# Vision tower on one core: scores of attention in the feed-forward before it, values behind them in another bank pair

## The chip, the cores and the metric

The kernel runs on one core of a Trainium2 chip. The metric is the time of one execution on the device, in microseconds (us). It was run three times: 1611.28, 1611.56 and 1613.82 us, median 1611.56. A profiled execution is a fourth one.

## What is computed

64 images (2 channels, 104x104) become 170 tokens of 128 numbers each (169 patches of 8x8 and a class token), and go through three stages. The reference, cut to what matters (helpers and reshapes left out):

```python
h = tok(x, gamma, beta, W, b)               # normalise 5 shifted copies, 8x8 convolution
h = concatenate([cls_tok, h], axis=1)       # 170 tokens per image
h = h + graph(layernorm(h), ...)            # two graph convolutions over 128 features, projection Wp
h = h + block(layernorm(h), ...)

def block(x):                               # 2 heads of 64, 8 experts of 512
    hx = layernorm(x) * ln_g + ln_b
    q, k, v = hx @ Wq, hx @ Wk, hx @ Wv     # per head
    q, k = l2norm(q) * 8 * qn_g, l2norm(k) * 8 * kn_g
    attn = softmax(where(causal, q @ k.T / 8, lowest))
    y = (attn @ v) @ Wo
    gate = softmax(y @ gate_W + gate_b)
    hid = gelu(y @ W1[e] + b1[e])           # for each of 8 experts, all tokens
    return sum_e gate[e] * (hid @ W2[e] + b2[e])
```

## The kernel before

The features lie on the 128 partitions, the tokens on the free axis. After the convolutions of all images, the 64 images are worked off in 16 groups of 4 (`NB`), 680 tokens each. A group passes a front end (second normalisation, graph, queries and keys), the attention and the feed-forward part. The front end of a group runs inside the feed-forward part of the groups in front of it, so one loop turn holds the feed-forward part of group g-1, the queries and keys of g, the start of g+1, and then the attention of g.

The feed-forward part has 32 slots (`SLOTS`: 8 experts, 4 chunks of 128 hidden features). In a slot TensorE multiplies six fp16 matmuls of 340 columns into a bank pair of `hid_ps` (`experts_in`, L869), ScalarE applies gelu once or twice (L564, L569), VectorE casts and subtracts to get the high and low fp16 parts (L1211, L1213), and three slots later (`LAG`) TensorE multiplies six more into `eo_ps` (`experts_out`, L886). After each fourth chunk VectorE weighs the expert's result with its gate (L1225, two halves) and GpSimd's queue adds it to the output in DRAM (L401). Slots 32 to 34 have no `experts_in` left. Fixed tables (`LN2_SLOTS`, `GATE_SLOTS`, `QK_SLOTS`, `EARLY_SLOTS`) say in which slot each front-end step runs. Every engine executes its own list in that order; semaphores join them.

PSUM is cut into four pairs of banks: two are `hid_ps`, one is `eo_ps`, one (`fr_ps`) belongs to the front end. `fr_ps` is last read in the feed-forward part by ScalarE's four relus of the next group but one (L485, slots 28 to 31), and the graph's products (`graph`, steps "plain" and 0 to 3, through `both`, L664) write it during the attention.

TensorE's order around the attention of group g is: `values` (L768) of two tokens' tiles at a time, in slots 32, 33, 34 and once more after them, each block of six fp16 matmuls into a quarter of `hid_ps`; `scores` of samples 0 and 1 (L783, and the mask, L787), which wait until ScalarE has copied the values of their bank out (`values_evac`, L518); "plain" and graph product 0 of group g+1; `scores` of samples 2 and 3; graph products 1 and 2; the transposes of the probabilities (`turn_probs`, L798) of samples 0 and 1; graph product 3; then weighing (`weigh`, L810), transposes and the projection (`project`, L817) by turns, the mean of the graph's result, and the gate logits (L853).

VectorE's order: the last expert's weighing in slot 34, then `maxima` of samples 0 and 1 and of 2 and 3 (two reductions, L1120, and nbias, L1123), `normalise` (L1128, L1135) of samples 0 and 1, the copy of the turned probabilities (`turned`, L1142) of sample 0, and so on by turns. ScalarE copies the values out, then runs 16 exponentials (`exps`, L528), each with a read of its sum.

In group 0 nothing lies in front of the attention (`later` is false), in group 15 there is no next group's graph (`ahead` is false).

Of the kernel before, what the change touches and what calls it, by code (L numbers as in the profile page):

```python
# [36 lines left out]
NB = 4  # L37
# [44 lines left out]
def vit_tower(nc, cells1, cells0, pack_a, pack_b, edge, w1, w2, out):  # L82
    with ExitStack() as ctx:
# [326 lines left out]
        def _(act):  # L410
# [100 lines left out]
                                         root[:, 2 * TILES:4 * TILES].unsqueeze(2).broadcast_to([QC, H * TILES, DH]),  # L511
                                         ACT.Copy).then_inc(wide_ready, 1)

            def values_evac(g, b, later):
                act.wait_ge(vp_ps, g * NB + b + 1)
                if b == 0 and later:
                    act.wait_ge(tmp_ready, g * E - 1)
                nc.scalar.activation(vp[:, b * 2 * D:(b + 1) * 2 * D], hid_ps[b // 2][0:QC, b % 2, 0:2 * D],  # L518
                                     ACT.Copy).then_inc(vp_ready, 1)

            def exps(g, b):

                act.wait_ge(nb_ready, g * (NB // 2) + b // 2 + 1)
# [18 lines left out]
                nc.scalar.activation(y32[:, j * TH:(j + 1) * TH], hid_ps[1][:, j, 0:TH], ACT.Copy).then_inc(y_ready, 1)  # L542

            def attention(g, later, ahead):
                for b in range(NB):
                    values_evac(g, b, later)
                for b in range(NB):
                    exps(g, b)
                nc.scalar.activation(primer[:, :], eps[0:1, 0:1], ACT.Gelu_apprx_tanh)
                o_evac(g, 0)  # L550
                y_evac(g, 0)
                o_evac(g, 1)
                y_evac(g, 1)
                if ahead:
                    graph(g + 1, "sq2")
                act.wait_ge(lg_step, 3 * (g + 1))
                nc.scalar.activation(lge[:, :], lg[:, :], ACT.Tanh, scale=0.5).then_inc(lge_ready, 1)
# [46 lines left out]
        def _(pe):  # L604
# [103 lines left out]
                    pe.wait_ge(xnl_ready, g + 1)  # L708
                    of_xn(adj_h[:, :], adj_l[:, :]).then_inc(g_ps, 1)

            def graph(g, step):
                if step == "plain":
                    pe.wait_ge(h1_ready, 4 * (g + 1))
                    of_xn(plain_h[:, :], plain_l[:, :], stop=False)
                if step in range(4):
                    last = both(gcn_m[:, step * D:(step + 1) * D], two(h1[:, step * T:(step + 1) * T]),
                                start=False, stop=(step == 3))
                    if step == 3:
                        last.then_inc(gcn_ps, 1)
                if step == "mean2":  # L720
                    pe.wait_ge(h2_ready, g + 1)
                    both(mean_m[:, :], tokens(g)).then_inc(mean2_ps, 1)
                if step == "var2":
                    pe.wait_ge(sq2_ready, g + 1)
                    means(sq).then_inc(var2_ps, 1)
                if step == "cast":
                    cast_roots(g, "ln2")
# [28 lines left out]
                if step == "cast":  # L756
                    cast_roots(g, "qk")

            def values(g, b, later):

                if b == 0 and later:
                    pe.wait_ge(hhi_act, his(g, 0) - 1)
                if b == 2 and later:
                    pe.wait_ge(hhi_act, his(g, 0))
                for k in range(2):
                    t = 2 * b + k
                    for n, (x_part, w_part) in enumerate(((xh_h, wv_h), (xh_l, wv_h), (xh_h, wv_l))):
                        last = mm(hid_ps[b // 2][0:QC, b % 2, k * D:(k + 1) * D],  # L768
                                  x_part[:, t * QC:(t + 1) * QC], w_part[:, :], start=(n == 0), stop=(n == 2))
                last.then_inc(vp_ps, 1)  # L770

            def scores(g, m):

                if m == 0:
                    pe.wait_ge(kn_ready, g + 1)
                pe.wait_ge(vp_ready, g * NB + 2 * m + 2)
                for b in (2 * m, 2 * m + 1):
                    ps = score_ps_at(b)
                    for c in range(2):
                        w = (c + 1) * QC  # L780
                        for h in range(H):
                            p = slice(h * DH, (h + 1) * DH)
                            mm(ps[:, h, c * QC:c * QC + w], qs[p, (2 * b + c) * QC:(2 * b + c + 1) * QC],  # L783
                               kb[p, b * TOK:b * TOK + w], start=(b == 2 * m and c == 0), stop=False)
                for h in range(H):
                    corners = hid_ps[m][0:QC, h, 0:2 * 3 * QC].rearrange("p (i j n) -> p i j n", i=2, j=3)[:, :, 0:3:2, :]
                    last = mm(corners, identb[:, :], mask[:, :].unsqueeze(1).unsqueeze(1).broadcast_to([QC, 2, 2, QC]),  # L787
                              start=False, stop=True)
                last.then_inc(score_ps, 1)
# [12 lines left out]
            def weigh(g, b):  # L802

                pe.wait_ge(pt_ready, g * NB + b + 1)
                for k in range(2):
                    for h in range(H):
                        v0 = b * 2 * D + k * D + h * DH
                        p0 = h * 3 * QC + k * TOK
                        y0 = (b % 2) * TOK
                        last = mm(hid_ps[0][h * DH:(h + 1) * DH, b // 2, y0 + k * QC:y0 + TOK], vp[:, v0:v0 + DH],  # L810
                                  pt[b % 2][0:QC, p0:p0 + TOK - k * QC], start=(k == 0), stop=(k == 1))
                last.then_inc(pv_ps, 1)
# [11 lines left out]
            def attention(g, later, ahead):  # L824
                def graph_of(*steps):
                    if ahead:
                        for step in steps:
                            graph(g + 1, step)

                for b in range(LAG if later else 0, NB):  # L830
                    values(g, b, later)
                scores(g, 0)
                graph_of("plain", 0)
                scores(g, 1)
                graph_of(1, 2)
                turn_probs(g, 0, later)
                turn_probs(g, 1, later)
                graph_of(3)
# [53 lines left out]
            def ffn(g, ahead):  # L892
                for slot in range(SLOTS + LAG):
                    if slot < SLOTS:
# [7 lines left out]
                        if ahead:  # L902
                            for step in steps_in(EARLY_SLOTS, slot):
                                early(g + 2, step)
                    else:
                        values(g + 1, slot - SLOTS, True)
                    if slot >= LAG:
                        experts_out(g, slot - LAG)

# [27 lines left out]
        def _(dve):  # L937
# [206 lines left out]
            def y_parts(g, j):  # L1144
# [4 lines left out]
                dve.wait_ge(yh_ready, 2 * g + j + 1)  # L1149
                v.tensor_tensor(yl[:, half], y32[:, half], yh[:, half], ALU.subtract).then_inc(yl_ready, 1)  # L1150

            def attention(g, later, ahead):
                maxima(g, 0)
                maxima(g, 1)
                normalise(g, 0)
                normalise(g, 1)
                turned(g, 0)
# [76 lines left out]
            def ffn(g, successor=True, ahead=True, later=True):  # L1234
                for slot in range(SLOTS + LAG):
                    expert_slot(g, slot, later)
                    for step in steps_in(GATE_SLOTS, slot):
                        gates(g, step, later)
                    if successor:
                        for step in steps_in(LN2_SLOTS, slot):  # L1240
                            graph(g + 1, step)
                        for step in steps_in(QK_SLOTS, slot):
                            queries_keys(g + 1, step)
                    if ahead:
                        for step in steps_in(EARLY_SLOTS, slot):
                            early(g + 2, step)
# [70 lines left out]
```

## Time and profile before

| what | value |
|---|---|
| three runs, median | 1611.56 us |
| profiled execution | 1615.64 us, its span 1613.8 us |
| TensorE (PE) busy | 1495.1 us, 93% of the span |
| VectorE (DVE) busy | 1211.3 us, 75% |
| ScalarE (ACT) busy | 1099.5 us, 68% |
| GpSimd (POOL) busy | 227.3 us, 14% |
| mean granted TensorE clock | 0.963 of full speed |

The span is what the profiler saw between the first and the last instruction; the time holds what lies around it as well. "Busy" counts every instruction from its start to its end; TensorE's instructions overlap and their ends are modelled, so a TensorE that is always busy need not be at its peak. A timeline merges instructions of one line that follow each other: the number behind the x says how many. A square bracket at a row's end says how long the engine was idle before it and what ended that. PEld is TensorE's loading of weights. The granted clock is 1.00 at full speed (2.4 GHz) and 0.50 at half. An fp32 matmul shows as two matmul instructions.

### The profile page before, as it was taken

What the parts mean: (1) busy time and instruction counts of PE and PEld (TensorE: products, weight loads), DVE (VectorE), ACT (ScalarE), POOL (GpSimd) and SP (SyncE); (2) the same over time, 40 slices, a digit from 0 to 9 for tenths busy, and PEclk for the clock granted to TensorE, in tenths of its full rate; (3) what the DMA queues carried; (4) which work ended last, traced back from release to release, by engine and by line L of the source; (5) the groups of instructions that cost most, each with busy time, mean ns of one, the idle gap of its engine ahead of it and who ended that gap; (6) DMA issues with size and microseconds to landing.
All of it is one profiled execution on the core that took longest, in us unless ns stands there. A gap on an engine that the chain in (4) does not pass through costs nothing.

```text
span 1613.8 us, 31251 instructions
## 1 busy us (share of the span) xinstructions
PE 1495.1 (93%) x10837; PEld 1020.8 (63%) x10837; DVE 1211.3 (75%) x2510; ACT 1099.5 (68%) x1879; POOL 227.3 (14%) x213
## 2 busy tenths in 40 slices
PE   5993589999999999999999999999999999999998
PEld 3551356666666666666666666666666666667665
DVE  7994358787868778787878787887878787877665
ACT  2321157777777777777777777777777777777766
POOL 5376101010110101010101101010101010110101
PEclk8995589999999999999999999999999999999979
DMA  5312004243333333241423333233324242433323
GB/s 189 116 65 79 9 5 110 36 104 43 97 51 95 42 89 52 59 80 26 112 35 104 43 95 47 92 43 91 49 45 94 33 109 38 104 43 97 53 88 53
DMA packets 33714, 113.48 MB, mean 70 GB/s; under 512 B 5008, under 2 KB 5008, under 8 KB 31120
## 3 DMA queue, kind: packets, MB, share of 16 engines
q0 software_dynamic: 18432, 44.57, 20.5%
q1 hardware_dynamic: 14960, 67.71, 11.4%
q10 hardware_dynamic: 288, 0.77, 0.1%
q8 instruction: 18, 0.29, 0.1%
q14 instruction: 16, 0.13, 0.0%
HBM read 62.56 MB, written 50.48 MB: 70 GB/s over the span
## 4 chain that ended last, share of the span: by engine, by line
PE 59%; DVE 28%; issue 7%; ACT 4%; DVEq 1%; DMA 1%; POOL 0%; POOLq 0%; ACTq 0%
PE pair L886 20%; PE pair L869 17%; PE pair L664 7%; DVE area L1213 5%; PE pair L650 4%; DVE area L1135 3%; DVE root_t L1055 2%; PE pair L783 2%; DVE area L1142 2%; DVE area L1225 2%; PE pair L692 1%; PE pair L676 1%; PE pair L817 1%; PE pair L739 1%; PE pair L810 1%
## 5 line engine op out<-in xcount | busy, mean ns | idle before, releaser
L564 ACT ACTIVATE area<-pair,pack_b_sb 128x680 f32<-128x680 f32 x512 | 422.8, 828 | 220.4 <-PE pair L869 217.8
L1213 DVE TENSOR_TENSOR area<-area 128x680 f16<-128x680 f32 x512 | 441.1, 864 | 149.3 <-ACT area L569 143.8
L886 PE MATMUL pair<-area,ws 128*128 128x340 f16 x3072 | 529.8, 307 | 12.9 <-DVE area L1225 11.8
L869 PE MATMUL pair<-area,ws 128*128 128x340 f16 x3072 | 527.1, 308 | 0.0
L886 PEld LDWEIGHTS pair<-area,ws 128*128 128x128 f16 x3072 | 284.3, 98 | 168.8 <-DVE area L1225 44.1
L869 PEld LDWEIGHTS pair<-area,ws 128*128 128x128 f16 x3072 | 297.8, 98 | 143.7 <-issue 0.2
L569 ACT ACTIVATE area<-pair,pack_b_sb 128x680 f16<-128x680 f32 x384 | 316.4, 824 | 0.0
L401 POOL DMA_DIRECT2D tower_out<-area x128 | 109.7, 857 | 1266.8 <-DVE area L1225 1205.3
L1225 DVE SCALAR_TENSOR_TENSOR area<-pair,pack_b_sb,area 128x340 f32<-128x340 f32 x256 | 134.0, 565 | 28.9 <-PE pair L886 19.9
L528 ACT ACTIVATE area<-pair,nbias,root 85x85 f32<-85x85 f32 (+1 forms) x256 | 112.4, 464 | 22.4 <-DVE nbias L1123 22.4
L650 PE MATMUL pair<-area,pack_a_sb 128*128 128x512 f32 (+1 forms) x260 | 97.1, 533 | 18.4 <-DVE area L1006 18.4
L650 PEld LDWEIGHTS pair<-area,pack_a_sb 128*128 128x128 f32 x260 | 50.7, 198 | 62.5 <-issue 42.9
L664 PE MATMUL pair<-area,gcn_m 128*128 128x340 f32 x256 | 83.4, 461 | 0.0
L1120 DVE TENSOR_REDUCE mx<-pair 85x4 f32<-85x340 f32 x64 | 41.0, 680 | 55.8 <-PE pair L787 55.8
L1006 DVE TENSOR_TENSOR area<-area,pack_a_sb 128x832 f32<-128x832 f32 x65 | 75.1, 1218 | 7.7 <-DMA pack_a_sb<-pack_a 6.3
L1211 DVE CAST area<-area 128x680 f16<-128x680 f32 x128 | 65.6, 513 | 19.7 <-ACT area L564 14.4
L451 ACT ACTIVATE ht<-pair 128x832 f32<-128x832 f32 x13 | 22.5, 1730 | 75.9 <-PE pair L650 75.9
L485 ACT ACTIVATE area<-pair,pack_b_sb 128x680 f32<-128x680 f32 x64 | 59.2, 935 | 20.2 <-PE pair L664 19.7
L373 POOL TENSOR_TENSOR area<-area 128x896 f32<-128x896 f32 x13 | 57.0, 4383 | 39.0 <-DMA area<-cells 38.0
L664 PEld LDWEIGHTS pair<-area,gcn_m 128*128 128x128 f32 x256 | 47.4, 195 | 18.0 <-issue 1.4
L798 PE MATMUL pair<-ident,area 85*85 85x85 f32 x384 | 45.4, 256 | 13.4 <-DVE area L1135 13.4
L1135 DVE TENSOR_SCALAR area<-area,rs 85x85 f32<-85x85 f32 (+1 forms) x256 | 55.7, 278 | 2.3
(182 smaller groups left out, 1640.7 us busy)
## 6 DMA issues: line engine op xcount, KB each, us to landing
tower_out<-area POOLq DMA_DIRECT2D x128, 340.0 KB, 4.6
area<-gate_scratch SPq DMA_DIRECT2D x16, 1360.0 KB, 9.9
area<-gate_scratch SPq DMA_DIRECT2D x16, 1020.0 KB, 7.1
area<-cells SPq DMA_DIRECT2D x14, 448.0 KB, 3.7
tower_out<-ht SPq DMA_DIRECT2D x16, 340.0 KB, 2.3
area<-gate_scratch SPq DMA_DIRECT2D x16, 340.0 KB, 4.4
area<-cells SPq DMA_DIRECT2D x13, 416.0 KB, 4.3
area<-w SPq DMA_DIRECT2D x1, 2048.0 KB, 10.1
```

The source lines that it names most:

```text
L401: pool.dma_start(out[:, g * T:(g + 1) * T], tmp[e % 2], accum_op=ALU.add).then_inc(out_done, 16)
L528: nc.scalar.activation(probs[:, b * SCORE + o0:b * SCORE + o0 + w], score_ps_at(b)[:, h, c * QC:c * QC + w], ACT.Exp, bias=nbias[:, n:n + ...
L564: nc.scalar.activation(two(hid[slot % NHID]), halves(hid_ps[slot % 2]), ACT.Gelu_apprx_tanh, bias=col(COL_B1 + slot)).then_inc(hid_ready, 1)
L569: nc.scalar.activation(two(hh[slot % NPART]), halves(hid_ps[slot % 2]), ACT.Gelu_apprx_tanh, bias=col(COL_B1 + slot)).then_inc(hhi_act, 1)
L650: last = mm(flat(conv_ps(p))[:, a:b], conv_w[:, s * D:(s + 1) * D], xg[p % 2][s][:, a:b], start=(s == 0), stop=(s == SHIFTS - 1))
L664: last = mm(fr_ps[:, j, 0:TH], lhs, rhs[:, j, :], start=start, stop=stop)
L869: last = mm(hid_ps[slot % 2][:, j, 0:TH], lhs[:, w], rhs[:, j * TH:(j + 1) * TH], start=(i == 0), stop=(i == 2))
L886: last = mm(eo_ps[:, j, 0:TH], lhs[:, w], rhs[:, j * TH:(j + 1) * TH], start=(m % CH == 0 and i == 0), stop=(m % CH == CH - 1 and i == 2))
L1006: v.tensor_tensor(xg[p % 2][s].rearrange("p (j b) -> p j b", b=B), src[:, c0 * B:(c0 + NP) * B].rearrange("p (j b) -> p j b", b=B), gv, AL ...
L1135: last = v.tensor_scalar(p, p, rs[:, n:n + 1], None, ALU.mult)
L1213: v.tensor_tensor(hl[slot % NPART], hid[slot % NHID], hh[slot % NPART], ALU.subtract).then_inc(hlo_ready, 1)
L1225: v.scalar_tensor_tensor(tmp[e % 2][:, j * TH:(j + 1) * TH], eo_ps[:, j, 0:TH], b2_s[:, e:e + 1], gbc[:, e * T + j * TH:e * T + (j + 1) * ...
```

## The change

The functions `scores` and `maxima` of group g+1 are now called in slots 32 and 33 of the feed-forward part of group g, where `values` stood on TensorE. All four blocks of values are made in the attention itself, behind slot 34, in `fr_ps` instead of `hid_ps`, once the relus have read it. VectorE (`values_out`) copies them out in two copies of 85x512 behind the last expert's weighing, where ScalarE had four copies of 85x256. "plain" waits for these copies, and so does each weighing. The scores wait for ScalarE's second gelu of slot 30 or 31 instead of for the values. In group 0 the scores and maxima of all samples stand ahead of the values.

```diff
--- before.py
+++ after.py
@@ -511,13 +511,6 @@
                                          root[:, 2 * TILES:4 * TILES].unsqueeze(2).broadcast_to([QC, H * TILES, DH]),
                                          ACT.Copy).then_inc(wide_ready, 1)
 
-            def values_evac(g, b, later):
-                act.wait_ge(vp_ps, g * NB + b + 1)
-                if b == 0 and later:
-                    act.wait_ge(tmp_ready, g * E - 1)
-                nc.scalar.activation(vp[:, b * 2 * D:(b + 1) * 2 * D], hid_ps[b // 2][0:QC, b % 2, 0:2 * D],
-                                     ACT.Copy).then_inc(vp_ready, 1)
-
             def exps(g, b):
 
                 act.wait_ge(nb_ready, g * (NB // 2) + b // 2 + 1)
@@ -542,8 +535,8 @@
                 nc.scalar.activation(y32[:, j * TH:(j + 1) * TH], hid_ps[1][:, j, 0:TH], ACT.Copy).then_inc(y_ready, 1)
 
             def attention(g, later, ahead):
-                for b in range(NB):
-                    values_evac(g, b, later)
+                if later:
+                    act.wait_ge(tmp_ready, g * E - 1)
                 for b in range(NB):
                     exps(g, b)
                 nc.scalar.activation(primer[:, :], eps[0:1, 0:1], ACT.Gelu_apprx_tanh)
@@ -708,9 +701,11 @@
                     pe.wait_ge(xnl_ready, g + 1)
                     of_xn(adj_h[:, :], adj_l[:, :]).then_inc(g_ps, 1)
 
-            def graph(g, step):
+            def graph(g, step, after=False):
                 if step == "plain":
                     pe.wait_ge(h1_ready, 4 * (g + 1))
+                    if after:
+                        pe.wait_ge(vp_ready, 2 * g)
                     of_xn(plain_h[:, :], plain_l[:, :], stop=False)
                 if step in range(4):
                     last = both(gcn_m[:, step * D:(step + 1) * D], two(h1[:, step * T:(step + 1) * T]),
@@ -756,24 +751,23 @@
                 if step == "cast":
                     cast_roots(g, "qk")
 
-            def values(g, b, later):
-
-                if b == 0 and later:
-                    pe.wait_ge(hhi_act, his(g, 0) - 1)
-                if b == 2 and later:
-                    pe.wait_ge(hhi_act, his(g, 0))
+            def values(g, b, ahead):
+
+                if b == 0 and ahead:
+                    pe.wait_ge(h1_ready, 4 * (g + 2))
                 for k in range(2):
                     t = 2 * b + k
                     for n, (x_part, w_part) in enumerate(((xh_h, wv_h), (xh_l, wv_h), (xh_h, wv_l))):
-                        last = mm(hid_ps[b // 2][0:QC, b % 2, k * D:(k + 1) * D],
+                        last = mm(fr_ps[0:QC, b // 2, (2 * (b % 2) + k) * D:(2 * (b % 2) + k + 1) * D],
                                   x_part[:, t * QC:(t + 1) * QC], w_part[:, :], start=(n == 0), stop=(n == 2))
                 last.then_inc(vp_ps, 1)
 
-            def scores(g, m):
+            def scores(g, m, later):
 
                 if m == 0:
                     pe.wait_ge(kn_ready, g + 1)
-                pe.wait_ge(vp_ready, g * NB + 2 * m + 2)
+                if later:
+                    pe.wait_ge(hhi_act, his(g, 0) - 1 + m)
                 for b in (2 * m, 2 * m + 1):
                     ps = score_ps_at(b)
                     for c in range(2):
@@ -802,6 +796,7 @@
             def weigh(g, b):
 
                 pe.wait_ge(pt_ready, g * NB + b + 1)
+                pe.wait_ge(vp_ready, 2 * g + b // 2 + 1)
                 for k in range(2):
                     for h in range(H):
                         v0 = b * 2 * D + k * D + h * DH
@@ -825,14 +820,14 @@
                 def graph_of(*steps):
                     if ahead:
                         for step in steps:
-                            graph(g + 1, step)
-
-                for b in range(LAG if later else 0, NB):
-                    values(g, b, later)
-                scores(g, 0)
-                graph_of("plain", 0)
-                scores(g, 1)
-                graph_of(1, 2)
+                            graph(g + 1, step, after=True)
+
+                if not later:
+                    for m in range(NB // 2):
+                        scores(g, m, later)
+                for b in range(NB):
+                    values(g, b, ahead)
+                graph_of("plain", 0, 1, 2)
                 turn_probs(g, 0, later)
                 turn_probs(g, 1, later)
                 graph_of(3)
@@ -902,8 +897,8 @@
                         if ahead:
                             for step in steps_in(EARLY_SLOTS, slot):
                                 early(g + 2, step)
-                    else:
-                        values(g + 1, slot - SLOTS, True)
+                    elif slot - SLOTS < NB // 2:
+                        scores(g + 1, slot - SLOTS, True)
                     if slot >= LAG:
                         experts_out(g, slot - LAG)
 
@@ -1149,9 +1144,16 @@
                 dve.wait_ge(yh_ready, 2 * g + j + 1)
                 v.tensor_tensor(yl[:, half], y32[:, half], yh[:, half], ALU.subtract).then_inc(yl_ready, 1)
 
+            def values_out(g, k):
+                dve.wait_ge(vp_ps, g * NB + 2 * k + 2)
+                v.tensor_copy(vp[:, k * 4 * D:(k + 1) * 4 * D], fr_ps[0:QC, k, :]).then_inc(vp_ready, 1)
+
             def attention(g, later, ahead):
-                maxima(g, 0)
-                maxima(g, 1)
+                if not later:
+                    for m in range(NB // 2):
+                        maxima(g, m)
+                for k in range(NB // 2):
+                    values_out(g, k)
                 normalise(g, 0)
                 normalise(g, 1)
                 turned(g, 0)
@@ -1234,6 +1236,8 @@
             def ffn(g, successor=True, ahead=True, later=True):
                 for slot in range(SLOTS + LAG):
                     expert_slot(g, slot, later)
+                    if successor and 0 <= slot - SLOTS < NB // 2:
+                        maxima(g + 1, slot - SLOTS)
                     for step in steps_in(GATE_SLOTS, slot):
                         gates(g, step, later)
                     if successor:
```

## Rows read from the trace of the kernel before

**Rows 1.** The page, part 4: shares of the chain that ended last, by engine.
```profile
PE 59%; DVE 28%; issue 7%; ACT 4%; DVEq 1%; DMA 1%; POOL 0%; POOLq 0%; ACTq 0%
```
**Rows 2.** Timeline of PE, first transposes of groups 1 and 14 (start, duration, what).
```profile
310.41 0.68 PE L798 MATMUL pair<-ident,area 85*85 85x85 f32 x6 [0.35 <-DVE area L1135]
...
1451.80 0.68 PE L798 MATMUL pair<-ident,area 85*85 85x85 f32 x6 [0.41 <-DVE area L1135]
```
**Rows 3.** Timeline of PE around the attention of group 8.
```profile
736.62 1.03 PE L886 MATMUL pair<-area,ws 128*128 128x340 f16 x6
737.48 0.27 PE L768 MATMUL pair<-wv_h,area 128*85 128x128 f16 x2
...
737.82 1.03 PE L886 MATMUL pair<-area,ws 128*128 128x340 f16 x6
...
743.03 0.75 PE L664 MATMUL pair<-pack_a_sb,plain_h 128*128 128x340 f16 x4
...
745.14 1.12 PE L783 MATMUL pair<-area 64*85 64x85 f32 x16
...
746.51 2.45 PE L664 MATMUL pair<-area,gcn_m 128*128 128x340 f32 x8
749.37 0.68 PE L798 MATMUL pair<-ident,area 85*85 85x85 f32 x6 [0.41 <-DVE area L1135]
...
754.88 0.66 PE L810 MATMUL pair<-area 85*64 85x170 f32 x8 [0.33 <-DVE area L1142]
...
759.98 1.89 PE L869 MATMUL pair<-area,ws 128*128 128x340 f16 x12
```
**Rows 4.** Waits of PE: total us, times, longest us.
```profile
PE pair L798 <- DVE area L1135: 13.4, 32, 3.1
```
**Rows 5.** Timeline of DVE around the attention of group 8.
```profile
739.42 0.87 DVE L1213 TENSOR_TENSOR area<-area 128x680 f16<-128x680 f32 x1 [1.38 <-ACT area L569]
741.09 1.05 DVE L1225 SCALAR_TENSOR_TENSOR area<-pair,pack_b_sb,area 128x340 f32<-128x340 f32 x2 [0.79 <-DMA tower_out<-area]
...
746.71 1.28 DVE L1120 TENSOR_REDUCE mx<-pair 85x4 f32<-85x340 f32 x2 [2.00 <-PE pair L787]
...
748.15 0.17 DVE L1128 RECIPROCAL rs<-sm 85x4 f32<-85x4 f32 x1
...
750.15 0.68 DVE L1142 COPY area<-pair 85x510 f32<-85x510 f32 x1
...
754.15 1.27 DVE L1142 COPY area<-pair 85x510 f32<-85x510 f32 x2
```
**Rows 6.** Timeline of ACT, group 8: the first exponential.
```profile
744.74 0.42 ACT L528 ACTIVATE area<-pair,nbias,root 85x85 f32<-85x85 f32 x1 [1.30 <-DVE nbias L1123]
```
**Rows 7.** Timelines of PE, then DVE, around the attention of the last group.
```profile
1521.71 1.03 PE L886 MATMUL pair<-area,ws 128*128 128x340 f16 x6
...
1532.73 0.96 PE L798 MATMUL pair<-ident,area 85*85 85x85 f32 x6 [3.11 <-DVE area L1135]
...
1538.74 1.16 PE L798 MATMUL pair<-ident,area 85*85 85x85 f32 x6
1539.83 1.12 PE L810 MATMUL pair<-area 85*64 85x170 f32 x8
...
1547.59 0.73 PE L869 MATMUL pair<-area,ws 128*128 128x340 f16 x2
...
1531.59 0.17 DVE L1128 RECIPROCAL rs<-sm 85x4 f32<-85x4 f32 x1 [0.47 <-ACT area L528]
```
**Rows 8.** Busy time by stretch: us, PE, PEld, DVE, ACT, POOL, then PEclk, DMA share, GB/s.
```profile
1534.00:1538.00 4.00, 3.52 (x22) 2.93 (x24) 3.77 (x15) 3.98 (x15) 0.00 (x0) 0.50 0.00 0
...
1550.00:1560.00 10.00, 10.00 (x60) 6.00 (x58) 6.38 (x12) 7.70 (x11) 0.00 (x0) 0.83 0.19 73
```
**Rows 9.** Timeline of PE in the attention of group 0.
```profile
213.93 1.12 PE L783 MATMUL pair<-area 64*85 64x85 f32 x16 [1.64 <-ACT area L518]
...
223.20 0.68 PE L798 MATMUL pair<-ident,area 85*85 85x85 f32 x6 [0.28 <-DVE area L1135]
```

## The prediction

> **What bounds the kernel now.** I read the chain of waits on the page first: TensorE carries 59% of it, VectorE 28%, ScalarE 4% [rows 1]. A change that only takes work off ScalarE is therefore worth nothing; what counts is when TensorE gets its next matmul. Then I read the timelines around one attention, that of group 8. Groups 1 to 14 run the same code under another group's feed-forward part, and their timelines repeat every 87.8 us (first transposes at 310.41 in group 1, at 1451.80 in group 14, 13 groups later) [rows 2], so one stands for 14. The reader should see in it that TensorE hardly rests: it waits 0.41 us ahead of the first transposes of the probabilities and 0.33 us ahead of the third weighing [rows 3]; with the second transposes, VectorE's normalisation made TensorE wait 32 times, 13.4 us in all, 3.11 of them at once in the last group [rows 4, 7]. VectorE, on the other hand, idles for 2.00 us ahead of the second pair of maxima, because the scores come late, and from there on it runs without a break: maxima, nbias, two normalisations, the copy of the turned probabilities, and so on to the third copy, which releases the third weighing [rows 5]. That copy at 754.15 sets the rest: third weighing at 754.88, next feed-forward at 759.98 [rows 3].
>
> **What moves.** The scores of group g+1 go from after the values into slots 32 and 33 of the feed-forward before it; their maxima on VectorE follow the subtraction of slot 31. The values go behind slot 34, into the front end's bank pair, and VectorE instead of ScalarE evicts them, in two copies of 85x512. TensorE's matmuls are the same in number and shape; only their order changes. VectorE gets 1.3 us of copies more per group, ScalarE loses four short ones, worth nothing, since its next work (the exponentials) waited for nbias. The graph's "plain" product now waits for both copies, and behind it on TensorE's queue stand all transposes and weighings, for which VectorE in turn waits.
>
> **TensorE's side, group 8.** Spacings: an output block 0.86, a values block 0.34 (737.48 to 737.82), scores of two samples 1.37 (745.14 to 746.51), plain and the first graph product 2.11 (743.03 to 745.14) [rows 3]; plain alone, six fp16 matmuls like a block, 0.87, so a graph product 1.24. The new order from 737.48: scores, block, scores, block, block, four values blocks, which is 737.56 + 1.38 + 0.87 + 1.37 + 0.87 + 0.87 + 1.34 = 744.3 (0.08 is put in for the first fp32 weights). The scores' banks are free in time: the subtraction of slot 31, which waits for ScalarE's last read of slot 31, starts at 739.42 [rows 5], the second scores at 739.8. Their results are there for VectorE at 739.1 and 741.4.
>
> **VectorE's side, group 8.** A busy VectorE starts the next instruction about 0.08 before the modelled end (two copies in 1.27, one in 0.68) [rows 5]. The subtraction of slot 31 starts at 739.42, so the first maxima start at 740.20. A pair of maxima with nbias costs 1.44 (746.71 to 748.15): 741.64, 743.08. Then come the last weighing of the experts, 0.97 (1.05 less the overlap): 744.05, and the copies, 0.60 and 0.68: 744.65 and 745.33. All inputs are there earlier by 0.25 us or more, except the last values block (744.5 against 744.65). So VectorE's queue, not TensorE, releases "plain", at 745.38: TensorE stalls 1.1 us where it had none. The price of a copy of 85x512 from PSUM is taken from the copies of 85x510 [rows 5], the same shape but for two columns.
>
> From 745.38 on: plain and product 0, 1, 2 take 0.87 + 3.53 (three fp32 pairs; eight matmuls in 2.45, four more at their spacing of 0.285) and the first transposes start at 749.78 instead of 749.37. The probabilities have been normalised since 746.3, because the first exponential moves from 744.74 [rows 6] to 741.7; the wait of 0.41 and that of the second transposes are gone. But VectorE's first copy of turned probabilities needs them turned: 749.78 + 0.72 (their modelled 0.68 and 0.04 of signal) = 750.50, where it started at 750.15 [rows 5]. The second normalisation, which used to fill that time, is done; the third and fourth stand behind the copies in VectorE's order and move with them. So the third copy, the third weighing and everything behind them come 0.34 us later. Early scores buy VectorE 3.2 us of idling ahead of that copy and nothing else. **Per group +0.34, 14 times: +4.8 us.** Bounds: +0.2 if the instructions overlap more than assumed; +0.5 if each of the seven VectorE instructions on that chain takes 0.02 more. An added satisfied wait ahead of each weighing is taken at nothing: the transposes already have two waits in one place, and each weighing's second wait was met 5 us before.
>
> **The last group** has no graph to cover the softmax. TensorE waits 3.11 us for the first transposes, and the granted clock, full before, falls to 0.50 (1.2 GHz) right after; it is back in the stretch from 1550 to 1560, whose mean of 0.83 puts the return near 1553.4 [rows 7, 8]. Counted from the block of chunk 28 at 1521.71 [rows 7], scores and values lie as above; VectorE's chain (second maxima when the scores are there, 4.77 later; then 1.44, 0.97, 0.60, 0.60) frees it at 1530.1, against 1531.59 for the first normalisation now. First transposes: 1.14 later, 1531.2 (from 1532.73), so TensorE idles about 1.8 us. After that the order normalise, turn, copy runs back to back instead of at the exponentials' pace. At the low clock transposes and weighings cost near 1.1 each (1538.74 to 1539.83) [rows 7], which puts the third weighing at about 1537.0 instead of 1539.83. **-2.8 us**, bounds -2.2 and, by the clock, -10.5 (below).
>
> **The first group** (nothing in front) loses its wait for the values' eviction: scores at 213.93 now, after a wait of 1.64 [rows 9] and four values blocks (2.6 at the half clock, estimate), so from 209.7 in the new order. It gets the two copies ahead of "plain". With scores at 1.4 (full clock) or 2.4 (estimate, half clock, by the ratio seen in the last group) each, the first transposes land between 221.1 and 225, now 223.20 [rows 9]. I take **-1.0**, bounds -2.3 and +1.7.
>
> **Sum:** 4.8 - 2.8 - 1.0 = +1.0 us. The profiled execution took 1615.64 (span 1613.8), so by it 1616.6; the median of the runs is 4.1 lower, and the forecast against it is 1611.56 + 1.0 = 1612.6. What a measurement of this kernel can tell from no change is about 0.2%, 3.2 us.
>
> **Rivals.** (B) The clock holds in the last attention. TensorE's idle stretch shrinks from 3.11 to about 1.8 us. At full speed the third weighing comes at 1536.05 and the last feed-forward 3.85 later (as from 754.88 to 759.98, less one fp32 pair, 1.24), 1539.9 against 1547.59: -7.7; the half clock's 5.8 us inside that feed-forward give back 2.9 more. 4.8 - 10.6 - 1.0 gives 1604.8. Against it: the transposes after the gap come one by one with rests between, and in the first group a rest of under 2 us (ahead of 213.93) [rows 9] was followed by slow matmuls too: from those scores to the transposes 9.3 us pass, where group 8 takes 7.7 for the same work. The Trainium skill, "TensorE: Matmul & The Clock Gate", section "Why this matters for your kernels", says that short gaps keep the clock up and that only longer ones bring it down; by that rule this rival, not my forecast, would hold. 0.20.
> (C) The copies don't hold TensorE: if VectorE got through its queue 1.1 us sooner, the first copy of turned probabilities would start at 749.4, -0.77 a group: -10.8 - 3.8, 1597.0. Nothing in the rows shortens the chain, and the reductions have the same shapes: 0.07.
> (D) Slower: the chain subtraction 31, maxima, maxima, weighing, copies, copies is longer than its rows elsewhere, since it now reads PSUM while ScalarE runs exponentials in the same pairs and TensorE writes. Every 0.1 us on it goes undiminished to "plain", 14 times. It decides from 0.25 us on; at 10% of its 5.1 us, a group costs 0.84: 11.8 - 3.8 = +8.0, 1619.6. For it: slacks of 0.1 to 0.4 us only. 0.20. The skill's "VectorE: DVE Perf Modes" says in its opening table that ScalarE sits closer to PSUM; that speaks against handing evictions to VectorE, and no run here shows by how much.
> (E) Nothing moves, because the scores' new places wait for ScalarE or kn so long that the old order returns: 1611.6. kn is computed in slot 15 and ScalarE is done 0.4 us earlier: 0.03.
>
> **Chances.** Forecast 0.50 (own range 1608.8 to 1618: middle groups 2.8 to 7.0, last -2.2 to -3.3, first -2.3 to +1.7). Its upper end lies past 1614.8 with 0.08, its lower past 1608.3 with 0.02. Faster: 0.20 + 0.07 + 0.02 = 0.29. Slower: 0.20 + 0.08 = 0.28. Same: 0.43. The range reaches into B and D: 1604 to 1619.5.
>
> **What would show it.** In the profile after: a wait of about 1.1 us on TensorE ahead of "plain" in groups 1 to 14, released by VectorE's values copy; no wait ahead of the first two transposes; VectorE idle about 3.2 us ahead of the first copy of turned probabilities; a period of 88.1 instead of 87.8; the wait ahead of the third weighing grown from 0.33 to about 0.7; in the last group an idle stretch near 1.8 us and the clock at 0.50 after it. A period under 87.6 or full clock after 1533 would prove me wrong.

## The result, and the profile after

The changed kernel takes 1624.91 us (median of six runs, 1621.53 to 1625.72) against 1611.57 before: the ratio of the runs is 1.0074, 95% interval 1.0061 to 1.0087. It is slower, by 0.7%, where 1612.6 was forecast.

These runs lie in two clusters for either kernel, near 1611.4 and 1613.9 before, 1621.7 and 1625.3 after, and of all executions behind this document one (2206.82 us, at a mean clock of 0.643, in before_half_idle) is left out everywhere. The profiled execution after took 1621.91 (span 1620.1), which is in its lower cluster; the one before took 1615.64, 1.8 above its upper one.

From the page after: the busy times, and the shares of the chain that ended last.

```profile
PE 1492.6 (92%) x10837; PEld 1020.5 (63%) x10837; DVE 1227.1 (76%) x2542; ACT 1079.4 (67%) x1815; POOL 227.1 (14%) x213
...
PE 54%; DVE 27%; issue 9%; ACT 7%; DVEq 1%; DMA 1%; POOL 0%; ACTq 0%; POOLq 0%
```

VectorE has 32 instructions and 16 us more, ScalarE 64 fewer and 20 us less, as the diff says. TensorE's busy time is 2.5 us less and does not show why the kernel is slower; the timeline does. Here is TensorE around the same attention after the change, the rows that answer to [rows 3]. (The prediction calls it group 8; counted from 0, as the first and the last are, it is group 6, and nothing hangs on that.)

```profile
736.64 1.03 PE L881 MATMUL pair<-area,ws 128*128 128x340 f16 x6
737.60 1.12 PE L777 MATMUL pair<-area 64*85 64x85 f32 x16
...
739.93 1.12 PE L777 MATMUL pair<-area 64*85 64x85 f32 x16
...
744.22 0.28 PE L761 MATMUL pair<-wv_h,area 128*85 128x128 f16 x2
...
745.52 0.74 PE L657 MATMUL pair<-pack_a_sb,plain_h 128*128 128x340 f16 x4 [0.97 <-DVE area L1149]
...
749.81 1.07 PE L792 MATMUL pair<-ident,area 85*85 85x85 f32 x12
...
755.29 0.88 PE L805 MATMUL pair<-area 85*64 85x170 f32 x8 [0.82 <-DVE area L1137]
756.10 1.50 PE L812 MATMUL pair<-area,pack_b_sb 128*128 128x340 f32 x2
757.54 1.12 PE L805 MATMUL pair<-area 85*64 85x170 f32 x8
```

The scores stand where the diff puts them, "plain" waits 0.97 us for the values' copy, the first two transposes run together without a wait, and the third weighing waits 0.82 instead of 0.33 us. What follows it was not in the forecast: the projection (L812) and the fourth weighing take about twice their usual time. The same stretches of VectorE, to be set beside [rows 5]:

```profile
739.44 0.87 DVE L1215 TENSOR_TENSOR area<-area 128x680 f16<-128x680 f32 x1 [1.38 <-ACT area L562]
740.22 1.27 DVE L1115 TENSOR_REDUCE mx<-pair 85x4 f32<-85x340 f32 x2
...
743.13 1.05 DVE L1227 SCALAR_TENSOR_TENSOR area<-pair,pack_b_sb,area 128x340 f32<-128x340 f32 x2
744.09 1.27 DVE L1149 COPY area<-pair 85x512 f32<-85x512 f32 x2
...
750.47 0.69 DVE L1137 COPY area<-pair 85x510 f32<-85x510 f32 x1 [3.12 <-PE pair L792]
```

VectorE runs without a break from 739.44 through both copies and two normalisations to 747.35, then idles 3.12 us ahead of the first copy of turned probabilities, which starts at 750.47. The next lines give TensorE's granted clock by stretch (length in us, busy times of PE, PEld, DVE, ACT, POOL, then the clock, DMA share and GB/s): all of groups 1 to 14, then three places in it.

```profile
240.00:1500.00 1260.00, 1214.28 (x9346) 843.12 (x9345) 981.26 (x2123) 921.97 (x1573) 118.07 (x128) 0.99 0.33 69
...
312.00:318.00 6.00, 6.00 (x18) 3.34 (x17) 1.71 (x3) 1.00 (x2) 0.00 (x0) 0.50 0.00 0
...
756.00:762.00 6.00, 6.00 (x20) 3.38 (x17) 1.59 (x3) 1.00 (x2) 0.00 (x0) 0.50 0.00 0
...
1288.00:1294.00 6.00, 6.00 (x22) 3.45 (x19) 1.49 (x4) 1.00 (x2) 0.00 (x0) 0.50 0.00 0
```

And before:

```profile
240.00:1500.00 1260.00, 1225.56 (x9452) 849.64 (x9451) 977.92 (x2118) 950.39 (x1643) 119.21 (x129) 1.00 0.34 69
```

In three of the 14 groups, right behind the wait ahead of the third weighing (groups 1, 6 and 12; the one at 755.29 is group 6's), the clock falls to half (1.2 GHz) for 6.8 us. Its price can be read from the first transposes of neighbouring groups:

```profile
661.62 1.07 PE L792 MATMUL pair<-ident,area 85*85 85x85 f32 x12
...
749.81 1.07 PE L792 MATMUL pair<-ident,area 85*85 85x85 f32 x12
...
841.15 1.07 PE L792 MATMUL pair<-ident,area 85*85 85x85 f32 x12
...
929.35 1.07 PE L792 MATMUL pair<-ident,area 85*85 85x85 f32 x12
```

The distances are 88.19, 91.34 and 88.20 us: a loop turn costs 88.20 (87.80 before), this one with a fall 3.1 more, and the three with a fall 3.05 more in the mean.

**Where the time went**, from the two traces, between the starts of the feed-forward parts of groups 0 and 14: 1243.2 us after against 1228.5 before (228.96 to 1472.2, and 233.89 to 1462.4). That is 14.7 us, of them 14 x 0.40 = 5.6 by the longer turn and 9.1 by three falls of the clock. The first group, from its "edges" product to its feed-forward part, takes 23.42 us (205.54 to 228.96) instead of 25.89 (208.00 to 233.89), -2.5; the last, from the feed-forward part of group 14 to its own, 82.3 (to 1554.4) instead of 85.2 (to 1547.6), -2.9.

### The profile page after: what moved, and what is told of

Same layout as the page of the kernel before. It is cut to its first block, busy times and chain, and to the rows that moved or that the text cites. A ratio compares the mean times of both kernels' runs of the same rounds, so it can differ in the third digit from the quotient of the medians.

```text
span 1620.1 us, 31281 instructions
## 1 busy us (share of the span) xinstructions
PE 1492.6 (92%) x10837; PEld 1020.5 (63%) x10837; DVE 1227.1 (76%) x2542; ACT 1079.4 (67%) x1815; POOL 227.1 (14%) x213
## 4 chain that ended last, share of the span: by engine, by line
PE 54%; DVE 27%; issue 9%; ACT 7%; DVEq 1%; DMA 1%; POOL 0%; ACTq 0%; POOLq 0%
PE pair L881 16%; PE pair L864 15%; PE pair L657 10%; DVE area L1215 5%; PE pair L805 3%; ACT area L562 2%; DVE area L1001 2%; DVE root_t L1050 2%; ACT area L557 2%; DVE mx L1115 2%; DVE area L1227 2%; PE pair L792 2%; PE pair L643 2%; PE pair L812 2%; PE pair L685 1%
## 5 line engine op out<-in xcount | busy, mean ns | idle before, releaser
L1227 DVE SCALAR_TENSOR_TENSOR area<-pair,pack_b_sb,area 128x340 f32<-128x340 f32 x256 | 133.9, 565 | 14.7 <-PE pair L881 14.3
L657 PE MATMUL pair<-area,gcn_m 128*128 128x340 f32 x256 | 79.9, 456 | 0.0
L1137 DVE COPY area<-pair 85x510 f32<-85x510 f32 x64 | 42.2, 679 | 46.3 <-PE pair L792 46.3
L535 ACT ACTIVATE area<-pair 128x340 f32<-128x340 f32 x32 | 14.5, 453 | 67.2 <-PE pair L812 67.2
```

Of the source, the lines that this page charges most:

```text
L657: last = mm(fr_ps[:, j, 0:TH], lhs, rhs[:, j, :], start=start, stop=stop)
L1227: v.scalar_tensor_tensor(tmp[e % 2][:, j * TH:(j + 1) * TH], eo_ps[:, j, 0:TH], b2_s[:, e:e + 1], gbc[:, e * T + j * TH:e * T + (j + 1) * ...
```

## The experiments

Theory 1: the clock falls because TensorE's wait ahead of the third weighing has grown from 0.33 to 0.82 us. Theory 2: it falls by the new wait of 0.97 us ahead of "plain", or by the new order as such. Every kernel is compared with the kernel before, by runs on the same chip; a turn is the distance of the first transposes of neighbouring groups in its profile, where no fall lies between.

**norms_first**: the changed kernel with

```diff
                 normalise(g, 1)
-                turned(g, 0)
                 normalise(g, 2)
-                turned(g, 1)
                 normalise(g, 3)
+                turned(g, 0)
+                turned(g, 1)
                 if ahead:
                     graph(g + 1, "h2")
```

> The changed kernel, but VectorE does the third and fourth normalisation ahead of the first copy of turned probabilities, in its idle 3.1 us. Theory 1 (the granted clock falls in some groups because TensorE's wait ahead of the third weighing has grown to 0.82 us): that wait is gone, no fall of the clock in groups 1 to 14, period 88.20 - 0.82 = 87.4 us; from the changed kernel without its three falls (1621.9 - 9.2 = 1612.7) less 14 x 0.82, so about 1601 to 1603. Theory 2 (the falls come from the 0.97 us wait ahead of 'plain', or from the new order as such): same period of 87.4 but 2 to 4 falls of 3.05 us each, 1608 to 1614.

Measured: 1604.47, ratio 0.9948 (0.9931 to 0.9965), 1.5 above the range given for theory 1; its last group takes 85.7 us where the changed kernel's takes 82.3, since its first copy now stands behind the normalisations of all samples. The turn is 87.31 us, the clock full from 240 to 1500, and the waits of TensorE in that stretch keep the one ahead of "plain" alone (engine, line, what it waited for; total us, times, longest):

```profile
PE pair L657 <- DVE area L1149: 13.6, 14, 1.0
```

**h2_later**: the changed kernel with

```diff
-                if ahead:
-                    graph(g + 1, "h2")
                 turned(g, 2)
+                if ahead:
+                    graph(g + 1, "h2")
                 turned(g, 3)
```

> The changed kernel, but VectorE's addition of the graph's result stands behind the third copy of turned probabilities instead of ahead of it. Theory 1: wait ahead of the third weighing falls from 0.82 to under 0.1 us, period 87.4, no falls of the clock in groups 1 to 14, about 1601. Theory 2: period 87.4, 2 to 4 falls, 1608 to 1614.

Measured: 1602.12, ratio 0.9933 (0.9916 to 0.9949), a turn of 87.37, full clock. Another edit that takes away the same wait takes away the falls too. Both keep the 0.97 us ahead of "plain" and the new order of scores and values, so theory 2 falls.

**values_slot34**: the changed kernel with

```diff
@@ TensorE, ffn
                     elif slot - SLOTS < NB // 2:
                         scores(g + 1, slot - SLOTS, True)
+                    else:
+                        for b in range(NB):
+                            values(g + 1, b, ahead)
@@ VectorE, ffn
                 for slot in range(SLOTS + LAG):
+                    if successor and slot == SLOTS + LAG - 1:
+                        for k in range(NB // 2):
+                            values_out(g + 1, k)
                     expert_slot(g, slot, later)
@@ both engines, attention
+                if not later:
...
```

(the last lines stand for the old places of `values` and `values_out`, which only group 0 keeps).

> The changed kernel, but the values stand in slot 34 ahead of the last output block, and their copies on VectorE ahead of the last expert's weighing. The wait of 0.97 us ahead of 'plain' goes, the 0.82 us wait ahead of the third weighing stays. Period 88.20 - 1.0 = 87.2 either way. Theory 1: 2 to 4 falls of the clock remain, 1612.7 - 14 + 9.2 = about 1608. Theory 2: no falls, about 1599.

Measured: 1614.57 (ten runs, 1612.01 to 1619.60), ratio 1.0012 (0.9999 to 1.0024). The wait ahead of "plain" is gone and the turn is 87.22, 0.98 less. The other wait stays, and so do the falls, now in seven places of groups 1 to 14 in its profile, more than in the changed kernel:

```profile
PE pair L805 <- DVE area L1141: 11.4, 14, 0.8
```

The profiled execution was the slowest of the ten (1619.6). Three of its seven turns with a fall are 1.6 us longer (the clock is down for 3.4 us), four are 3.1 us longer (6.8 us), 17 us in all. The forecast of 1608 was 6 us low, in part because I took two to four falls for given: without its 17 us this execution would still stand at 1602.5, where 1599 was expected.

This run also answers a rival that I had not named, that the clock falls with all of TensorE's waiting in a turn. Its listed waits from 240 to 1500 come to 30.9 us, less than the 33.3 of the kernel before, which has no fall there.

**before_plus_idle**: the kernel before with

```diff
                     graph(g + 1, "h2")
+                v.tensor_tensor(dev[:, 0:TH], xh[:, 0:TH], xh[:, 0:TH], ALU.subtract)
                 turned(g, 2)
```

> The kernel before, with one more VectorE subtraction of 128x340 (about 0.45 us, its result is used by nothing) ahead of the third copy of turned probabilities. Theory 1: TensorE's wait ahead of the third weighing grows from 0.33 to about 0.78, as in the changed kernel, and the clock falls in 2 to 4 of the groups 1 to 14: 1611.6 + 15 x 0.45 + 3 x 3.05 = about 1627. Theory 2: no falls, 1611.6 + 6.8 = 1618.4.

Measured: 1627.84, ratio 1.0090 (1.0071 to 1.0109). The wait brings the falls into the kernel that had none; here one of them, in TensorE's timeline, behind a weighing that waits 0.75 us,

```profile
757.50 0.93 PE L810 MATMUL pair<-area 85*64 85x170 f32 x8 [0.75 <-DVE area L1142]
758.37 1.50 PE L817 MATMUL pair<-area,pack_b_sb 128*128 128x340 f32 x2
```

and the clock in that stretch:

```profile
758.00:764.00 6.00, 6.00 (x22) 3.45 (x19) 1.37 (x4) 1.00 (x2) 0.00 (x0) 0.50 0.00 0
```

Two turns of the 14 are 91.4 us long, the others about 88.22: with the scores, the values and their copies all in the old places. Theory 1 is shown from both sides, by taking the wait away and by putting it in. The mean clocks of all executions say the same: every execution of a kernel with a wait of 0.75 us or more in that place has a mean clock of 0.954 to 0.962, every other one whose clock was recorded 0.963 to 0.968.

**before_half_idle**: the same line with `0:D` for `0:TH`.

> The kernel before with a smaller extra subtraction on VectorE (128x128, about 0.2 us) ahead of the third copy of turned probabilities: a wait of about 0.5 us, between 0.33 (no falls seen) and 0.8 (falls in two or more groups). Without falls 1611.6 + 15 x 0.2 = 1614.6; with falls of 3 us each in as many groups as before, 1621 to 1627. The theory that the clock falls with the length of this wait allows both and says that the limit lies between; a fall of the clock without any relation to the wait would have shown in the kernel before.

Measured: 1615.35 (median of nine runs), ratio 1.0016 (1.0006 to 1.0026), a turn of 88.00, and no fall of the clock from 240 to 1500:

```profile
240.00:1500.00 1260.00, 1222.94 (x9433) 847.83 (x9431) 978.05 (x2125) 948.07 (x1639) 119.19 (x129) 1.00 0.34 69
```

The wait of the third weighing in that stretch (total us, times, longest):

```profile
PE pair L810 <- DVE area L1142: 7.5, 14, 0.5
```

So 0.53 us in that place cost 0.2 a turn and no fall, and 0.75 cost falls on top.

**before_h2_later**: the kernel before with the edit of h2_later.

> The kernel before, with VectorE's addition of the graph's result behind the third copy of turned probabilities: that repair alone, without the new order of scores and values. The 0.33 us wait ahead of the third weighing goes: period 87.4, 15 x 0.37 less, about 1606. If that is so, most of what the repaired changed kernel gains in the middle groups has nothing to do with early scores, and the change itself is worth only its first and last group. If the wait only moves behind (to the fourth weighing or the mean), 1611.

Measured: 1605.30, ratio 0.9953 (0.9940 to 0.9966), a turn of 87.40. The 0.33 us wait was worth 0.40 a turn, and one moved call beats the kernel before by 0.5% without the change.

**both_repairs**: values_slot34 with the edit of norms_first.

> The changed kernel with both repairs: values in slot 34 with their copies ahead of the last expert's weighing, and all four normalisations ahead of the first copy of turned probabilities. If the two waits are separate costs they add up: period 88.20 - 0.98 - 0.89 = 86.3 us, no falls of the clock in groups 1 to 14, 1604.5 - 14 x 0.98 = about 1591. If another wait takes their place (VectorE's queue has less slack when TensorE comes sooner), the period stays at 86.8 or more, 1597 or more.

Measured: 1591.42, ratio 0.9864 (0.9848 to 0.9881), a turn of 86.33, full clock. The waits add up. TensorE around the attention of group 6, no wait left:

```profile
733.47 0.74 PE L657 MATMUL pair<-pack_a_sb,plain_h 128*128 128x340 f16 x4
...
737.77 1.07 PE L792 MATMUL pair<-ident,area 85*85 85x85 f32 x12
...
742.36 0.66 PE L805 MATMUL pair<-area 85*64 85x170 f32 x8
...
747.46 1.89 PE L865 MATMUL pair<-area,ws 128*128 128x340 f16 x12
```

This begins to answer what before_h2_later asked, what early scores are worth once nothing holds TensorE behind them; the next run, with the same repair as before_h2_later, gives the number.

**values_slot34_h2_later**: values_slot34 with the edit of h2_later.

> The changed kernel with values in slot 34 and the graph's addition behind the third copy (instead of all normalisations first). Middle groups as with both repairs, period 86.4, no falls of the clock; in the last group the first transposes need not wait for the fourth sample's exponentials (14.1 instead of 16.7 us from first transposes to the feed-forward), in the first group 0.9 less. About 1589, 1% to 1.6% under the kernel before and 2 under both repairs.

Measured: 1590.10, ratio 0.9852 (0.9838 to 0.9866), a turn of 86.40, full clock. Within its interval it is as fast as both_repairs; both are 1.4 to 1.5% under the kernel before. It differs from before_h2_later only by the new order with the values in slot 34, which is thus worth 87.40 - 86.40 = 1.00 us a turn. With the values where the change puts them the new order is worth next to nothing there: 87.40 - 87.37 = 0.03 (h2_later). So my expectation for before_h2_later, that early scores are worth little in the middle groups, was right for the change as it stands, and wrong once the values stand in slot 34.

**scalar_evicts**: the changed kernel with ScalarE's copies,

```diff
+                exps(g, 0)
+                for k in range(NB // 2):
+                    act.wait_ge(vp_ps, g * NB + 2 * k + 2)
+                    nc.scalar.activation(vp[:, k * 4 * D:(k + 1) * 4 * D], fr_ps[0:QC, k, :],
+                                         ACT.Copy).then_inc(vp_ready, 1)
-                for b in range(NB):
+                for b in range(1, NB):
                     exps(g, b)
```

and without `values_out` on VectorE.

> The changed kernel, but ScalarE copies the values out (two copies of 85x512, between the exponentials of the first and of the second sample) instead of VectorE. If VectorE's full queue sets the wait ahead of 'plain', it shrinks by some 0.4 us (the values are ready at 744.5, the last copy ends about 745.1 instead of 745.5), period 87.8, falls of the clock as in the changed kernel: about 1616. If the wait were set by TensorE's own values or by the order, 88.2 and 1622; if ScalarE's copies of 85x512 are slow or its delayed exponentials come due, more than 88.2.

Measured: 1625.42, ratio 1.0073 (1.0057 to 1.0088). The turn is 88.00, 0.2 less than with VectorE, not 0.4, and the time is 9 us above the 1616 forecast for a wait set by VectorE's queue. The wait ahead of "plain" is 0.77 us, behind two copies that take as long as VectorE's:

```profile
748.02 1.26 ACT L543 ACTIVATE area<-pair 85x512 f32<-85x512 f32 x2 [0.31 <-PE pair L766]
...
749.43 0.74 PE L662 MATMUL pair<-pack_a_sb,plain_h 128*128 128x340 f16 x4 [0.77 <-ACT area L543]
...
759.20 1.12 PE L810 MATMUL pair<-area 85*64 85x170 f32 x8 [0.81 <-DVE area L1142]
```

Most of that wait thus stays when another engine makes the copies; VectorE's full queue adds 0.2 us. The 0.81 us wait and the falls (four in groups 1 to 14 of its profile, one of them of 3.4 us) stay. The engine was a small matter, their place a larger one (0.98 a turn in values_slot34).

**changed_again**: the changed kernel, unaltered, profiled a second time.

> The changed kernel unaltered, profiled a second time. If its two clusters of times (1621.5 to 1621.9 and 1624.9 to 1625.7) differ by one fall of the clock, a profile of the upper cluster shows four low stretches of 6.8 us in groups 1 to 14 instead of three, at other groups, and the same period of 88.20 outside them. If the clusters differ in something else, the number of low stretches is three in both.

Measured: 1625.02, its profile from the upper cluster (1625.13, span 1623.3). It shows three falls again, in the same groups. So the clusters are not one fall apart, and the second of the two outcomes named came. This execution enters group 0 later: its "edges" product there starts at 208.3 instead of 205.5, its first transposes at 221.3 instead of 218.5, and the clock ahead of them is at half until 212 instead of 209. That is 2.7 of the 3.2 us between the two spans, and it lies ahead of everything that the change touches. The same step separates the profiles of the kernel before (208.0) and before_half_idle (205.6), whose front ends are alike. What makes it is not shown, and no execution of the kernel before from its lower cluster was profiled.

## Why the prediction was wrong

**The mechanism in the middle groups** held, piece by piece. "VectorE's queue, not TensorE, releases 'plain', at 745.38": 745.52, with a wait of 0.97 for the 1.1 forecast. First transposes at 749.78: 749.81. First copy of turned probabilities at 750.50: 750.47. VectorE idle 3.2 us ahead of it: 3.12. Wait ahead of the third weighing "about 0.7": 0.82. The turn grew by 0.40 for 0.34. What that wait ahead of "plain" is made of was only half right: in scalar_evicts, with the copies taken out of VectorE's queue, 0.77 of it is left, by TensorE's own values and two copies behind them.

**The step that failed** is the sum itself: it has the granted clock as a term of the last group only ("falls to 0.50 right after") and takes full clock for granted in groups 1 to 14, since before the change nothing fell there. The step "the third copy, the third weighing and everything behind them come 0.34 us later" prices the longer wait at its delay alone. It costs that (0.40 a turn), and in three of 14 groups 3.05 us more by the fall of the clock: 9.1 of the 9.9 us that the forecast lacks in the middle. Rival D named a slower outcome, 1619.6, but by another mechanism, VectorE's chain being longer than its rows; the chain's instructions were within 0.1 us of them, and "plain" within 0.14. No rival had the clock in a middle group.

**The first group** gave -2.5 for -1.0. The surplus comes from the kernel before as it was profiled. In it the clock, back at full at 212, fell once more from 215.4 to 218.8, behind the 1.64 us wait ahead of the scores (before_half_idle and before_plus_idle show the same fall, behind 1.64 and 1.70 us). The changed kernel has no wait between the first products and the scores and no such fall: it takes 23.42 us in one profile and 23.47 in the other, though the clock came back at 209 in one and at 212 in the other. The clock of the two kernels from 212 to 225, before, then changed_again:

```profile
212.00:225.00 13.00, 10.78 (x72) 6.99 (x71) 5.63 (x19) 10.05 (x36) 0.00 (x0) 0.87 0.00 0
...
212.00:225.00 13.00, 11.48 (x100) 8.47 (x100) 9.18 (x30) 11.43 (x37) 0.00 (x0) 0.99 0.00 0
```

In before_h2_later, whose group 0 differs from that of the kernel before by the moved call alone, the wait was 1.49 us, this fall did not come, and the first group takes 23.81. With 0.3 for its missing wait (an estimate, by the 0.33 of the other groups) that is 24.1 without the fall, and the change is worth -0.7 there.

**The last group** held: an idle stretch of 1.77 us for 1.8, half clock from 1544, and -2.9 for -2.8. Only the fall came 3 us behind the first transposes and not right after the rest. TensorE's timeline, then the clock by stretch:

```profile
1541.14 0.68 PE L792 MATMUL pair<-ident,area 85*85 85x85 f32 x6 [1.77 <-DVE area L1130]
```

```profile
1544.00:1557.00 13.00, 12.36 (x66) 8.48 (x65) 6.06 (x20) 4.50 (x9) 0.00 (x0) 0.50 0.00 1
```

**Rival B**, the clock holding in the last group, did not come. The rule quoted with it (the Trainium skill, "TensorE: Matmul & The Clock Gate", "Why this matters for your kernels": only longer idle gaps bring the clock down) is not borne out here: in the last group the clock fell behind a gap of 1.77 us and two of 0.31, and in the middle groups where the longest gap nearby is 0.82 us. What the Trainium skill says in "VectorE: DVE Perf Modes", "Specifications", that ScalarE sits closer to PSUM, does not show in scalar_evicts: two copies of 85x512 take 1.26 us on ScalarE and 1.27 on VectorE.

Set against the measured difference: like clusters compared, 1621.7 to 1611.4 and 1625.3 to 1613.9, it is 10.3 to 11.4 us. Forecast +1.0, plus 9.1 for the falls, plus 0.8 for the turn (14 x 0.06), less 1.5 and 0.1 for the first and the last group, gives 9.3. That is what the profiles show (spans of 1613.8 before and 1623.3 in changed_again, 9.5 apart). The missing 1 to 2 us stay open. They would be found if the usual executions of the kernel before lacked the extra fall in group 0 (with -0.7 for the first group instead of -2.5 the sum is 11.1), and the profiled one was 1.8 us slower than its upper cluster; but no other was profiled, and two kernels with the same group 0 up to one instruction show this fall too.

## What to carry to other kernels

When TensorE is busy almost all the time, look for the thin stretches in it (small transposes and weighings with rests between) and price a wait that grows there twice: once for itself, and once for the chance that the granted clock falls and everything behind it runs at half speed for several microseconds. Here 0.53 us was still free of that and 0.75 was not. Moving work earlier gained next to nothing (0.03 us a turn) while the values and their copies still stood between it and the next matmuls, and 1.00 us once they were moved too; after such a move, look at what now stands in the queues behind it. Here one moved call, with the values and their copies put ahead of the last output block and weighing, turned +0.7% into -1.5%; the moved call alone, without the change, gave -0.5%.

## What the runs showed of the hardware that was not expected

- The clock fell with no idle gap over 0.82 us near by; in values_slot34 this is the longest wait of TensorE anywhere from 240 to 1500. With 0.33 and 0.53 us in that place it never did in 14 groups; with 0.75 to 0.82 us it did in two to seven of them, in four kernels of different orders. A gap of 0.97 us ahead of "plain", amid dense matmuls, did no harm in norms_first and h2_later.
- Which groups are hit is not settled. In two profiles of the changed kernel they were the same three, and the number differed between kernels: three at a turn of 88.20 us, two at 88.22, four at 88.00 with ScalarE's copies, seven at 87.22. That the length of the turn sets it is not shown. Nor was it tried whether the gap counts by itself or only together with the thin work around it.
- A fall costs 3.05 us in the changed kernel for 6.8 us at half clock, and 1.6 us for the shorter ones of 3.4 us in values_slot34: somewhat under half of the low time. TensorE is busy in all of it (6.00 of 6.00 us in the three stretches shown).
